# Selective scan: both states of a pair in one scan, the first product of a row kept in SBUF

## The reference, cut to what matters

```
def _mamba_dir(xz, ...):                 # 256 channels d, 16 states n, length 512 l
    u     = _causal_conv_silu(x, conv_w, conv_b)
    x_dbl = einsum('bdl,kd->bkl', u, xproj_w)          # dt, B and C
    delta = softplus(einsum('dr,brl->bdl', dtproj_w, x_dbl[:, :r]) + dt_bias)
    dA    = exp(einsum('bdl,dn->bdln', delta, A))
    dBx   = einsum('bdl,bnl,bdl->bdln', delta, Bm, u)
    h     = scan over l of  h = dA * h + dBx
    y     = einsum('bdln,bnl->bdl', h, Cm) + Dp * u
    return y * silu(z)
out_f = _mamba_dir(xz, ...)
out_b = _mamba_dir(xz[:, :, ::-1], ...)[:, :, ::-1]    # backward
attn  = einsum('bdl,od->blo', out_f + out_b, out_proj_w)
ffn   = sum over the 4 chosen experts of gate * (gelu(x @ w1 + b1) @ w2 + b2)
return x + attn + ffn
```

## Time and profile before

| | us |
|---|---|
| median of 3 runs | 1092.48 (1090.7 to 1092.59) |
| the profiled execution | 1092.9 |
| its span, first to last record | 1091.1 |
| busy: VectorE / ScalarE / TensorE / GpSimd | 1029.2 / 940.0 / 932.0 / 907.3 |
| VectorE's scans L1581, 512 of 128x512 | 598.2 |
| GpSimd's products L851, 246 of 128x1024 | 527.0 |

### The profile page before, as it was taken

One profiled execution on the slowest core, in us unless ns is written; L12 is line 12 of the kernel. 1 busy time (PEld: TensorE's weight loads), 2 busy tenths in 40 slices (PEclk: granted clock), 3 DMA queues, 4 the chain that ended last, 5 costly groups with the idle time before them and its releaser, 6 DMA issues. The chain is left out here.

```text
span 1091.1 us, 21878 instructions
## 1 busy us (share of the span) xinstructions
PE 932.0 (85%) x5866; PEld 732.8 (67%) x5866; DVE 1029.2 (94%) x1361; ACT 940.0 (86%) x1755; POOL 907.3 (83%) x567
## 2 busy tenths in 40 slices
PE   5478888857789999989999889899999999988894
PEld 2233333326678788878878777788788878877783
DVE  7889999779999999999999989999999999988896
ACT  4258989979899999989999989899899989988950
POOL 4278888766689999999999998989999999988862
PEclk9678989778999999999999999999999999999996
DMA  9956676677566877787687767776877777666658
GB/s 305 377 191 242 241 280 226 225 267 233 177 176 181 233 197 187 205 218 196 165 225 196 201 171 219 205 192 180 238 191 185 211 210 201 164 167 170 188 114 243
DMA packets 153107, 228.87 MB, mean 210 GB/s; under 512 B 36300, under 2 KB 98028, under 8 KB 147700
## 3 DMA queue, kind: packets, MB, share of 16 engines
q1 hardware_dynamic: 125844, 208.39, 60.0%
q0 software_dynamic: 27136, 19.02, 12.3%
HBM read 161.84 MB, written 69.64 MB: 212 GB/s over the span
## 5 line engine op out<-in xcount | busy, mean ns | idle before, releaser
L1581 DVE TENSOR_TENSOR_SCAN arena<-arena,ps 128x512 f32<-128x512 f32 x512 | 598.2, 1202 | 2.8 <-issue 1.4
L851 POOL TENSOR_TENSOR arena<-arena 128x1024 f32<-128x1024 f32 x246 | 527.0, 2472 | 44.5 <-DVE arena L1581 44.4
L1081 ACT ACTIVATE arena<-delta,a_neg 128x511 f32<-128x511 f32 x512 | 341.3, 728 | 6.3 <-DVE arena L1581 3.2
L836 POOL DMA_INDIRECT acc_d<-yrows,tags x160 | 253.1, 1582 | 46.5 <-issue 36.8
L1257 PE MATMUL ps<-ident,arena 128*128 128x128 f32 x2048 | 270.6, 276 | 3.5 <-DVE arena L1589 3.5
L1569 DVE TENSOR_TENSOR ps<-du,ps 128x512 f32<-128x512 f32 x352 | 232.8, 677 | 18.0 <-PE ps L1321 15.9
L1257 PEld LDWEIGHTS ps<-ident,arena 128*128 128x128 f32 x2048 | 233.0, 142 | 15.6 <-DVE arena L1589 4.0
L817 POOL DMA_INDIRECT slots_d<-arena,pos x128 | 148.4, 1159 | 37.1 <-issue 35.1
L1286 PE MATMUL ps<-w,arena 128*128 128x128 f32 x1248 | 174.6, 283 | 3.0 <-ACT arena L1049 3.0
L1286 PEld LDWEIGHTS ps<-w,arena 128*128 128x128 f32 x1248 | 154.4, 192 | 12.8 <-issue 3.8
L1278 PE MATMUL ps<-rowsT,w 128*128 128x256 f32 x640 | 155.8, 387 | 8.3 <-ACT arena L1031 7.6
(11 more groups left out here) (154 smaller groups left out, 911.6 us busy)
## 6 DMA issues: line engine op xcount, KB each, us to landing
arena<-c_d SPq DMA_DIRECT2D x128, 512.0 KB, 4.2
w<-w_dram SPq DMA_DIRECT2D x80, 258.0 KB, 3.1
w<-w_dram SPq DMA_DIRECT2D x80, 256.0 KB
rows<-slots_d SPq DMA_DIRECT2D x80, 130.0 KB
slots_d<-delta SPq DMA_DIRECT2D x5, 2015.0 KB, 18.9
delta_d<-arena SPq DMA_DIRECT2D x8, 1024.0 KB, 4.9
du_d<-delta SPq DMA_DIRECT2D x8, 1024.0 KB, 7.9
delta<-delta_d SPq DMA_DIRECT2D x8, 1024.0 KB, 7.0
```

The lines of the kernel that those rows point to most:

```text
L836: pool.indirect_dma_start(acc_d[j % W_RING], bass.IndirectOffsetOnAxis(ap=tags[:, j, a, 0:1].bitcast(I32), axis=0), yrows[:, j % W_RING, a ...
L851: nc.gpsimd.tensor_tensor(state[:, q % H_RING], state[:, q % H_RING], c_rows[:, r % C_RING], ALU.mult).then_inc(s["prod_done"], 1)
L1081: nc.scalar.activation(decay[:, q % DA_RING, j, lo:lo + L - 1], delta[:, par, dh, lo:lo + L - 1], ACT.Exp, scale=a_neg[:, dh, 2 * g + j:2 ...
L1581: nc.vector.tensor_tensor_scan(state[:, q % H_RING, j, way], decay[:, q % DA_RING, j, way], b_ps[:, ROW[q, j], j, way], 0.0, ALU.mult, ALU ...
```

## The change

Four things change. (1) All backward pairs, and the forward pairs of the BOTH groups, are scanned in one instruction of 1024 elements over both states (`joined`); the other forward pairs keep two scans of 512. (2) The two states' products of a backward pair are made by one instruction of 1024 elements, `du` being broadcast over the states. (3) Of the two products that share a B row, the first one made (`beside`: the second forward pair of a group, the first backward one) goes into a new SBUF tensor `aside`, and its scan reads it there; the other is made in place in PSUM. The two forward products of a group stand together at its start. (4) With that the rows of `b_ps` are used in another order (`row`, `fill_freed`), and `gates` moves into the space of `rowsT`.

```
+def forward(q):
+    return q // NH % ND == 0
+def joined(q):
+    return not forward(q) or scaled(q, 0)
+DBX = [d for g in range(PAIRS // DH) for d in (() if g in BOTH else (DH * g + 1, DH * g)) + (DH * g + 2, DH * g + 3)]
...
+def row(q):
+    return (q // DH + (q % DH == 1)) % 2
+def fill_freed(q, j):
+    q = q - 3 if q % DH == 0 else q - 2
+    return 2 * q + 2 if joined(q) or q % NH or j == 0 else 2 * q + 1
 def scans_to(q, j):
-    return 2 * DH * (q // DH) + SCAN_ORDER.index((q % DH, j)) + 1
+    return 2 * q + 2 if joined(q) or j == q % NH else 2 * q + 1
+def beside(q):
+    return forward(q) == (q % NH == 1)
+def aside_free(q):
+    if forward(q):
+        return scans_to(q - 3, 1)
+    return scans_to(q - DH, 1) if joined(q - 1) else scans_to(q - 1, 0)
...
-        gates = sb("gates", [P, NT, TOPK])
+        aside = sb("aside", [P, 2, L])
+        gates = rowsT[:, 0:NT * TOPK].rearrange("p (t k) -> p t k", k=TOPK)
...
-                            wait(pe, s["scan_done"], DECAYS * b + scans_to(q - 2, j))
+                            wait(pe, s["scan_done"], DECAYS * b + fill_freed(q, j))
...
+                def dbx(q):
+                    base = q - q % NH
+                    own = slice(0, 1) if forward(q) else slice(0, 2)
+                    b_rows = b_ps[:, row(base), own, :]
+                    dve.wait_ge(s["b_ready"], len(FILLS) * b + fill_of(base, 0))
+                    if beside(q):
+                        wait(dve, s["scan_done"], DECAYS * b + aside_free(q))
+                    nc.vector.tensor_tensor(aside[:, own, :] if beside(q) else b_rows,
+                                            bc(du[:, par, q % DH, :].unsqueeze(1), [P, own.stop, L]), b_rows, ALU.mult).then_inc(s["dbx_done"], 1)
+                def scan_of(q, own):
+                    dve.wait_ge(s["decay_ready"], DECAYS * b + 2 * q + own.stop)
+                    by_vector = [j for j in range(own.start, own.stop) if not scaled(q, j)]
+                    if by_vector:
+                        dve.wait_ge(s["dbx_done"], len(DBX) * b + DBX.index(q) + 1)
                     else:
+                        dve.wait_ge(s["b_ready"], len(FILLS) * b + fill_of(q, own.start))
                     wait(dve, s["summed"], PAIRS * b + q - H_RING + 1)
+                    way = slice(None) if forward(q) else slice(None, None, -1)
+                    both = lambda ap: ap.rearrange("p j l -> p (j l)")[:, way]
+                    src = aside if by_vector and beside(q) else b_ps[:, row(q)]
+                    nc.vector.tensor_tensor_scan(both(state[:, q % H_RING, own]), both(decay[:, q % DA_RING, own]),
+                                                 both(src[:, own]), 0.0, ALU.mult, ALU.add).then_inc(s["scan_done"], own.stop - own.start)
+                def scan(q):
+                    if joined(q):
+                        scan_of(q, slice(0, 2))
+                    else:
+                        for j in (1, 0) if q % NH == 0 else (0, 1):
+                            scan_of(q, slice(j, j + 1))
...
                 for q in range(0, PAIRS, DH):
+                    if not scaled(q, 0):
+                        dbx(q + 1)
                     product(q - 1)
+                    if not scaled(q, 0):
+                        dbx(q)
+                    scan(q)
+                    scan(q + 1)
                     product(q)
+                    dbx(q + 2)
                     product(q + 1)
+                    dbx(q + 3)
+                    scan(q + 2)
                     if q == 0 and not first:
                         gate_batch(b - 1, 1 - par, i if par else i - 1)
+                    scan(q + 3)
                     product(q + 2)
```

More of the change, by code:

```diff
@@ L81 @@
 FILLS = [(q, j) for q in range(PAIRS) for j in (1, 0) if scaled(q, j) or q % NH == 0]
-DBX = [(q, j) for g in range(0, PAIRS, DH) for q, j in ((g, 0), (g + 1, 0), (g + 2, 1), (g + 2, 0), (g + 3, 0), (g + 3, 1))
-       if not scaled(q, j)]
+def forward(q):
[3 more added lines that the diff above has]
+DBX = [d for g in range(PAIRS // DH) for d in (() if g in BOTH else (DH * g + 1, DH * g)) + (DH * g + 2, DH * g + 3)]
 def fill_of(q, j):
     return 1 + FILLS.index((q, j) if scaled(q, j) else (q - q % NH, j))
[L91 to L100, removed]
-def scans_to(q, j):
-    return 2 * DH * (q // DH) + SCAN_ORDER.index((q % DH, j)) + 1
+def row(q):
[3 more added lines that the diff above has]
+    return 2 * q + 2 if joined(q) or q % NH or j == 0 else 2 * q + 1
+def scans_to(q, j):
+    return 2 * q + 2 if joined(q) or j == q % NH else 2 * q + 1
[5 more added lines that the diff above has]
+    return scans_to(q - DH, 1) if joined(q - 1) else scans_to(q - 1, 0)
 PROD_RING = 2
@@ L1311, in batch @@
                         if (q, j) in FILLS:
-                            wait(pe, s["scan_done"], DECAYS * b + scans_to(q - 2, j))
+                            wait(pe, s["scan_done"], DECAYS * b + fill_freed(q, j))
                             if scaled(q, j):
                                 pe.wait_ge(s["scaled"], 2 * (len(SCALED) * b + SCALED.index((g, j)) + 1))
-                                bank = b_ps[:, ROW[q, j], j, :]
+                                bank = b_ps[:, row(q), j, :]
                                 for t in range(TPB):
@@ L1320, in batch @@
                             else:
-                                last = nc.tensor.matmul(b_ps[:, ROW[q + 1, j], j, :], sel[:, 2 * g + j, :], parts[:, par, d, :],
+                                last = nc.tensor.matmul(b_ps[:, row(q), j, :], sel[:, 2 * g + j, :], parts[:, par, d, :],
                                                         start=True, stop=True)
@@ L1576, in scan @@
+                def scan_of(q, own):
[3 more added lines that the diff above has]
+                        dve.wait_ge(s["dbx_done"], len(DBX) * b + DBX.index(q) + 1)
                     else:
-                        dve.wait_ge(s["dbx_done"], len(DBX) * b + DBX.index((q, j)) + 1)
+                        dve.wait_ge(s["b_ready"], len(FILLS) * b + fill_of(q, own.start))
@@ L1579, in scan @@
                     wait(dve, s["summed"], PAIRS * b + q - H_RING + 1)
-                    way = slice(None) if q % DH < NH else slice(None, None, -1)
-                    nc.vector.tensor_tensor_scan(state[:, q % H_RING, j, way], decay[:, q % DA_RING, j, way],
-                                                 b_ps[:, ROW[q, j], j, way], 0.0, ALU.mult, ALU.add).then_inc(s["scan_done"], 1)
+                    way = slice(None) if forward(q) else slice(None, None, -1)
+                    both = lambda ap: ap.rearrange("p j l -> p (j l)")[:, way]
@@ L1592, in batch @@
                 for q in range(0, PAIRS, DH):
-                    dbx(q, 0)
+                    if not scaled(q, 0):
+                        dbx(q + 1)
                     product(q - 1)
-                    scan(q, 1)
-                    scan(q, 0)
-                    dbx(q + 1, 0)
+                    if not scaled(q, 0):
+                        dbx(q)
+                    scan(q)
+                    scan(q + 1)
                     product(q)
-                    scan(q + 1, 1)
-                    scan(q + 1, 0)
-                    dbx(q + 2, 1)
+                    dbx(q + 2)
                     product(q + 1)
[L1603 to L1606, removed]
+                    dbx(q + 3)
+                    scan(q + 2)
                     if q == 0 and not first:
                         gate_batch(b - 1, 1 - par, i if par else i - 1)
-                    dbx(q + 3, 1)
+                    scan(q + 3)
                     product(q + 2)
-                    scan(q + 3, 0)
-                    scan(q + 3, 1)
                 if isinstance(b, int) and b == BATCH - 1:
```

## The result

The changed kernel takes 1263.85 us (median of 4 runs, 1263.17 to 1265.85), the kernel before 1091.88 in the same comparison: ratio 1.158, 95% interval 1.156 to 1.160. The direction was the one forecast; the size was not. The forecast of 1169 us, with a range up to 1215, expected 77 us more, and 172 came. The profiled execution's span is 1261.6 us.

The account below looks back on a forecast made before the run. GpSimd was taken as the limit: 99.3 us a batch plus 12.6 of holding gives 111.9, +10.6 a batch. Six middle batches (63.6) and the ends sum to +76.7 on 1092.9, so 1169 us, range 1110 to 1215.

Parts of the forecast that it names:

- What bounds the kernel: Middle batches: GpSimd limits at 99.3 us of a 101.3 us batch, slack 2.0; VectorE needs 98.6.
- The sizes of joined instructions: VectorE: scan of 1024 takes 2.19 us (gain 0.05), joined product about 1.14 (gain 0.03); 1.5 us a batch.
- a scan with two SBUF inputs and a product exclude each other: VectorE scans reading `aside` and GpSimd products each held until the other ends; GpSimd loses 12.6 us a batch.
- the port of the rivals: Whatever a VectorE instruction with two SBUF inputs and a GpSimd product can't use together; no size of its own.
- and take turns when both queue: Queued `aside` scans and GpSimd products alternate: VectorE waits 0.63 us a scan, GpSimd sets 111.9 us a batch.
- rival B: GpSimd keeps the port through a run of products; +13.7 us a batch, 1193 us in all; chance 0.18.
- The upper end of 1252 us: Bound with all holding by `aside` scans put on GpSimd: 123.5 us a batch, some +159 us in all.
- the little that sticks out: Scan begun in a send holds GpSimd only past the send's end: 0.07 us short, 0.25 long.
- The waits costed at nothing: Joined products waiting for both fills of a row, and the other reorderings, were taken to cost nothing.
- rival C: Scans with two SBUF inputs don't hold GpSimd, which runs at 99.3 us a batch; 1080 us; chance 0.07.
- The cover named for them: VectorE's time to spare behind GpSimd hides the joined products' waits; without it, part of 10.1 us returns.
- Rival A: Scans and GpSimd products share the port element by element; +4.9 us a batch, 1128 us; chance 0.17.

Follow-up runs that it names:

- the control run: The kernel before, with GpSimd starting a product only when its own product before is done: 1113.96 us, ratio 1.020.
- the runs one by one: The changed kernel and the kernel before, each with GpSimd starting a product only when its own product before is done: 1233.75 and 1113.96 us.

## Why the prediction was wrong, point by point

- **What bounds the kernel.** That VectorE's saving alone gives back no more than GpSimd's slack fits the run without `aside`: VectorE's instructions are shorter in sum there, and the kernel is not faster. That GpSimd has little slack fits the control run: a short gap between its products cost 22 us. But VectorE had hardly more, as the run with two of the products moved to it shows.
- **The sizes of joined instructions** were about right, a little low. From start to start a scan of 1024 takes 636.59 to 638.77, 2.18 us (2.19 forecast, gain 0.06); a joined product 1.11 and 1.13 (1.14 forecast, gain 0.05). That is 20 x 0.06 + 16 x 0.05 = 2.0 us a batch against the 1.5 forecast.
- **That a scan with two SBUF inputs and a product exclude each other** held: in time (159 us with and without `aside`), in the rows (scans end one scan time after the run of products), and for reading alone (a fill of 1.8 us holds none). What it is that they exclude each other at, the port of the rivals, no run shows.
- **The step that failed: "and take turns when both queue".** From it came a VectorE wait of 0.63 us a scan and GpSimd as the limit at 111.9 us. No row and no run shows such turns between products that follow each other without a gap; they were an assumption of the author's. In fact GpSimd's products follow each other without letting the scan in (67 of the 69 held scans got in only at the end of the run of products). The short scans wait 2.90 us, the long ones 0.98, 25.3 us a batch in place of 8.8; GpSimd's products are hardly held (4 of 246 last over 2.7 us), and VectorE becomes the limit at 125.7 us. This is rival B, which had a chance of 0.18. The earlier trace rows already pointed to it, though L1382 there is a `tensor_scalar` with a single tensor input, an instruction of another kind, which no run here takes further. Its 1193 us were too low because its term, one more product for half of the held scans, was: 4.4 x 2 us plus 8.8 against the measured 25.3. The upper end of 1252 us bounded GpSimd's holding, not VectorE's, and so was no bound.
- **A term left out: the sends.** The sum let a scan that meets a send pass for the little that sticks out. A send beside such a scan lasts up to 3.6 us in place of 1.58. That matters where turns are taken: the forecast of 77 us for turns is 120 in the runs one by one, and the sends' 51 us are more than the difference. In the changed kernel itself VectorE is the limit, and the longer sends lie behind it.
- **The waits costed at nothing** cost some: without any holding the kernel was at 1105, not at the 1080 of rival C. The cover named for them, VectorE's time to spare behind GpSimd, did not hide them: there GpSimd's products wait longer for VectorE's scans. Which of the waits does it is open. These 13 us are measured with the first products in PSUM; in the changed kernel they can't be told from the rest.
- **Rival A** (shared element by element) is out: held scans wait for whole instructions (the one of 614.24 until the product that ends at 618.19), and products keep their 2.0 us.

No run here beats the kernel before.

## What to carry to other kernels

Before an operand is moved from PSUM to SBUF, count the tensor inputs of each VectorE instruction that lie in SBUF: with two, scans and `tensor_tensor` here waited for GpSimd's products (a scan of 2.27 us took up to 6.12, a `tensor_tensor` of 1.21 up to 2.67), with one in PSUM no scan exceeded 2.29 us (the run without `aside`); and 67 of 69 held scans waited for the end of a whole run of products, not of one instruction. The gain of joining two instructions was 0.05 us a pair here; the wait of a scan had a mean of 1.0 us (long) and 2.9 us (short), up to 4.1. And where two engines are equally loaded, cost the loser of a conflict both ways, since the side that waits decides which engine becomes the bound.

## What the runs showed of the hardware that was not expected

- GpSimd's queued products keep a waiting VectorE instruction out until the run ends (6.12 us for a scan of 2.27); with a gap of 0.08 to 0.24 us between products the means fell from 3.82 and 3.19 us to 2.06 and 2.97. The order is not that of the starts of the records: the scan of 614.24 began 1.38 us before the second product of the run (615.62), and that went first. When either of them is ready to read the trace doesn't show; a product's record begins some 0.6 us before the one ahead of it ends.
- A GpSimd indirect DMA is held by a VectorE scan with two SBUF inputs (3.62 us in place of 1.58), but does not hold it by itself: a scan beside a send keeps 2.28 us. Where a product followed the send without a gap, scans that began 0.4 us or more into the send waited for the end of that product (up to 5.35 us in the run one by one).
- A GpSimd fill, which only writes, holds no such scan (2.29 and 1.20 us beside fills of 1.8 us).
